# Four-layer transformer kernel: clipping moved from VectorE to GpSimd in a quantised layer, and matrix products of the identity added ahead of the first attention units of the last phase

## The reference

```python
def _act_fake_quant(x, clip_factor):
    scale = jax.nn.sigmoid(clip_factor) * jnp.max(jnp.abs(x)) / QMAX
    return jnp.clip(_ste_round(x / scale), -QMAX - 1.0, QMAX) * scale
...
xq = _act_fake_quant(x, clip_x[0])
gate = jnp.einsum('bsh,ih->bsi', xq, _weight_fake_quant(w_gate))
up = jnp.einsum('bsh,ih->bsi', xq, _weight_fake_quant(w_up))
h = _act_fake_quant(jax.nn.silu(gate) * up, clip_down[0])
return jnp.einsum('bsi,hi->bsh', h, _weight_fake_quant(w_down))
```

## Time and profile before

| what | value |
|---|---|
| runs, median of three | 2119.77 us |
| lowest and highest of them | 2115.42 and 2124.47 us |
| the profiled execution, its own time | 2117.64 us |
| its span, first to last instruction | 2115.9 us |
| PE busy | 1859.6 us, 88% of the span |
| DVE busy | 1486.2 us, 70% |
| ACT busy | 1302.6 us, 62% |
| POOL busy | 616.5 us, 29% |
| mean granted TensorE clock | 0.957 |

### The profile page before, as it was taken

The page is one execution under the profiler, slowest core; times in us unless marked ns, Lnnn a source line. Parts: engine busy times, 40 slices in busy tenths (PEclk is TensorE's granted clock), DMA queues, the critical chain, the costliest instruction groups (busy, mean ns, idle before and its releaser), DMA issues.

```text
span 2115.9 us, 49981 instructions
## 1 busy us (share of the span) xinstructions
PE 1859.6 (88%) x17665; PEld 1511.9 (71%) x17669; DVE 1486.2 (70%) x3873; ACT 1302.6 (62%) x4466; POOL 616.5 (29%) x610
## 2 busy tenths in 40 slices
PE   3998999989999897577898889999999998898879
PEld 2777888878888775455666677787777777677665
DVE  5898887878888785757666675767757565654556
ACT  1987766656667786456577766667666654544432
POOL 0003031322322220034333343254452523233321
PEclk9999999999999999868699999999999999999999
DMA  8013455444644001300000011222222223232351
GB/s 245 17 31 105 126 163 156 134 136 140 181 133 127 26 26 50 110 20 20 30 7 15 7 46 50 83 75 89 79 74 69 76 87 91 71 103 70 110 155 43
DMA packets 128789, 178.44 MB, mean 84 GB/s; under 512 B 10144, under 2 KB 89824, under 8 KB 128288
## 3 DMA queue, kind: packets, MB, share of 16 engines
q1 hardware_dynamic: 120864, 159.51, 25.0%
q0 software_dynamic: 7680, 15.74, 2.4%
HBM read 141.26 MB, written 33.95 MB: 83 GB/s over the span
## 4 chain that ended last, share of the span: by engine, by line
PE 38%; DVE 9%; ACT 6%; issue 4%; POOL 1%; DMA 0%; DVEq 0%; ACTq 0%; SPq 0%
PE ps L1674 5%; PE ps L1959 5%; PE ps L1907 3%; PE ps L1712 3%; PE ps L1900 3%; ACT pb L2108 3%; PE ps L1696 3%; PE ps L1881 2%; PE ps L1703 2%; PE ps L1685 2%; PE ps L1722 1%; DVE nm L2487 1%; PE ps L1730 1%; PE ps L1929 1%; PE ps L1873 1%
## 5 line engine op out<-in xcount | busy, mean ns | idle before, releaser
L2108 ACT ACTIVATE pb<-ps,nm 128x128 f32<-128x128 f32 x1024 | 363.1, 377 | 192.6 <-DVE nm L2487 192.5
L2156 POOL TENSOR_TENSOR pb<-pb,rcs 128x512 f32<-128x512 f32 x256 | 268.3, 1049 | 667.1 <-DVE rcs L2495 666.2
L986 ACT ACTIVATE pb<-pb,nm 128x128 f32<-128x128 f32 x1024 | 312.9, 393 | 30.9 <-DVE nm L1221 29.1
L2512 DVE COPY pt<-ps 128x512 f32<-128x512 f32 x128 | 88.3, 690 | 203.6 <-PE ps L1959 203.4
L2108 ACT ACTIVATION_READ_ACCUMULATOR pb<-ps,nm 128x1 f32 x1024 | 221.3, 216 | 0.0
L2487 DVE TENSOR_REDUCE nm<-ps 128x8 f32<-128x1024 f32 x128 | 155.9, 1218 | 62.2 <-PE ps L1907 39.0
L1959 PE MATMUL ps<-w,pb 128*128 128x128 f32 x1024 | 168.7, 290 | 21.9 <-ACT pt L2116 10.8
L1221 DVE TENSOR_REDUCE nm<-pb 128x8 f32<-128x1024 f32 x128 | 156.2, 1220 | 4.4
L1959 PEld LDWEIGHTS ps<-w,pb 128*128 128x128 f32 x1024 | 122.4, 148 | 46.3 <-ACT pt L2116 20.3
L870 PE MATMUL ps<-w,pb 128*128 128x128 f32 x1024 | 141.8, 280 | 8.2 <-ACT pb L986 7.9
L2116 ACT ACTIVATE pt<-ps 128x512 f32<-128x512 f32 x128 | 76.9, 601 | 94.9 <-PE ps L1959 94.6
(11 more groups left out here) (379 smaller groups left out, 4405.0 us busy)
## 6 DMA issues: line engine op xcount, KB each, us to landing
big<-in_we SPq DMA_DIRECT2D x92, 514.0 KB
big<-in_we SPq DMA_DIRECT2D x109, 384.0 KB
sorted_out<-big SPq DMA_DIRECT2D x27, 256.0 KB
big<-sorted_in SPq DMA_DIRECT2D x7, 960.0 KB, 5.7
sorted_in<-big SPq DMA_DIRECT2D x4, 1472.0 KB, 12.1
big<-sorted_in SPq DMA_DIRECT2D x20, 256.0 KB, 3.8
hidden<-h_all SPq DMA_DIRECT2D x7, 512.0 KB, 3.0
h_all<-hidden SPq DMA_DIRECT2D x7, 512.0 KB, 3.7
```

Source lines behind the costliest of these rows:

```text
L986: m = a.activation(pb[:, n % 2, k * S:(k + 1) * S], pb[:, n % 2, k * S:(k + 1) * S], ACT.Exp, bias=nm[:, n % 2, k:k + 1])
L2108: m = a.activation(pb[:, n % 2, e * S:(e + 1) * S], ps[:, score_bank(n) + half, k * S:(k + 1) * S], ACT.Exp, bias=nm[:, n % 2, e:e + 1], a ...
L2156: g_.tensor_tensor(p4, p4, r4.unsqueeze(2).to_broadcast([P, 4, S]), ALU.mult).then_inc(n2["p_normed"], 1)
L2512: v.tensor_copy(pt[:, p % 2, 4 * S:8 * S], ps[:, BANK_T, :]).then_inc(n2["p_lo"], 1)
```

## The change

The eight clips of the quantised layer leave DVE and become instructions of GpSimd, with the same bounds, the same wait for `x_copied` and the same signal; DVE's wait for `scales` ahead of the first clip goes too. In the third phase a second helper `idle_work` stands in PE's `work`, which issues products of the identity with itself into `BANK_PV` at four places of the first group: ten at `hs` -4, place 0, ahead of the down projection; fourteen at `hs` -3, place 2, ahead of the transposes of y; two at `hs` -2, place 0, ahead of the query projection; and five at `hs` -1, place 1, ahead of the scores of unit 0. They wait for nothing and signal nothing.

```diff
+            @block.gpsimd
+            def _(g_):
+                for j in range(NG):
+                    source = h_all[:, FF_ORDER[j] * NC1, :]
+                    g_.wait_ge(x_copied, j + 1)
+                    g_.tensor_scalar(source, source, MAGIC + QMAX, MAGIC - QMAX - 1.0, ALU.min, ALU.max).then_inc(quantised, 1)
...
-                def clipped(j):
-                    source = h_all[:, FF_ORDER[j] * NC1, :]
-                    v.wait_ge(x_copied, j + 1)
-                    v.tensor_scalar(source, source, MAGIC + QMAX, MAGIC - QMAX - 1.0, ALU.min, ALU.max).then_inc(quantised, 1)
...
-                v.wait_ge(scales, 2)
-                clipped(0)
                 for j, g in enumerate(FF_ORDER):
-                    if j + 1 < NG:
-                        clipped(j + 1)
                     for c, (at, m) in enumerate(CH1):
...
+                def idle_work(count):
+                    for k in range(count):
+                        pe.matmul(ps[:, BANK_PV, k % 4 * P:(k % 4 + 1) * P], ident, ident, start=True, stop=True)
+
                 def work(place, hs):
+                    if hs == L2_AT[0][0] - 4 and place == 0:
+                        idle_work(10)
+                    if hs == L2_AT[0][0] - 3 and place == 2:
+                        idle_work(14)
+                    if hs == L2_AT[0][0] - 2 and place == 0:
+                        idle_work(2)
+                    if hs == L2_AT[0][0] - 1 and place == 1:
+                        idle_work(5)
                     chunk = QK_AT.get(hs)
```

## The result

The changed kernel takes 2098.39 us, the median of 8 runs from 2092.44 to 2100.51. The kernel before, run beside it, takes 2115.57 us, the median of 8 runs from 2106.40 to 2124.47. The ratio is 0.993, with a 95% interval from 0.9913 to 0.9947.

The account below looks back on a forecast made before the run. Bounds: a DVE-ACT ring in the quantised layer's passes, and PE's waits and low clock at the third phase's start. 2117.64 - 9.2 (clips) - 1.1 (identity products) = 2107.3 us, taken as 2108; range 2102 to 2115.

Parts of the forecast that it names:

- The clips: Quantised layer: clips moved to POOL bring passes to 4.38 us, worth -9.2 us, between -8.4 and -9.2.
- the ring: Quantised layer: each pass loops through DVE and ACT (maxima, clip, `rounded`, silu, product, maxima), 5.91 us on average.
- PE's ring: Quantised layer: PE's three chunks, `turn`, ACT's `turned`, PE again; bounds a pass at 4.38 us after the change.
- The price of POOL's clip: Quantised layer: a clip on POOL taken as 0.8 us, covered in later passes; 0.89 us free at the first.
- The rival of a late first clip: Quantised layer: only POOL's first clip is late; 2108 us, or some 2113 with a 6 us first call; chance 0.05.
- a clip longer than a pass: Quantised layer: POOL's clip sets the pass, nothing won from 5.85 us a clip; 2129 us at 7.5; chance 0.03.
- POOL against DVE: Quantised layer: whether working POOL slows DVE's products or maxima; no loss taken, 3.1 us if held; rival's chance 0.08.
- The rival of passes of 4.82 us: Quantised layer: DVE and POOL hold each other, so passes cost 4.82 us; 2110.4 us; chance 0.08.
- The identity products: Start of third phase: raise PE's clock; +0.3 down projection, -0.5 transposes, -0.5 query projection, -0.4 scores: -1.1 us.
- bring nothing: Start of third phase: clock stays low or falls before the transposes; 0 to +2.5 us, 2109.4 us; chance 0.15.
- the clock stays up: Third phase: high clock lasts past the scores, some 6 us beyond the forecast, 2101 us; chance 0.09.
- How the numbers follow: Closing step giving chances and range; low-clock pieces between 934 and 1072 move, allowed 3 us either side.

Follow-up runs that it names:

- e5: Kernel before with the clip kept on DVE but issued a pass earlier, no identity products added: 2101.66 us, ratio 0.9932.
- e7: Changed kernel with two instead of three identity products behind each chunk of the quantised layer: 2102.54 us, ratio 0.9943.
- e2: Kernel before plus only the third-phase identity products, clips staying on DVE: 2121.16 us, ratio 1.0022.
- e8: Changed kernel with fourteen more identity products at `hs` 0 and five at `hs` 1, behind the first scores: 2096.59 us, ratio 0.9919.
- e1: Changed kernel without the third-phase identity products, so only the clips on POOL: 2100.29 us, ratio 0.9944.
- e12: Kernel before, unaltered, profiled a third time: 2114.21 us.
- e9: e1 plus five unread copies on DVE (about 0.9 us) ahead of the third phase: 2112.58 us, ratio 0.9999.
- e10: e1 plus twenty-two small unread copies on DVE (about 2.1 us) ahead of the third phase: 2111.80 us, ratio 0.9995.
- e3: Changed kernel again, unaltered: 2098.79 us, ratio 0.992.
- e6: Changed kernel with four unread copies on DVE (about 1.1 us) ahead of the third phase's first instruction: 2104.07 us, ratio 0.9945.
- e11: e7 and e8 together, on the changed kernel: 2093.23 us, ratio 0.9909.
- e4: Kernel before again, unaltered, a single execution: 2119.62 us.

## Why the prediction was wrong

**The clips: right, one figure by luck.** A pass of 4.38 us was forecast and 4.38 came; seven gave 9.16 us, forecast 9.2. The reason held in both halves: e5 shows that the place in order opened the ring, e7 that PE's ring is what remained. But the 4.38 us were read off the first step, and that step is ACT's. The timeline of ACT after the change has a load of 1.28 us there and `turned` right behind the silu, with no wait for PE; the last row is `turned` of a later pass, which waits for PE:

```profile
840.89 1.28 ACT L1328 ACT_TABLE_LOAD   x1
842.19 1.26 ACT L1328 ACTIVATE hT<-ps,gsc 128x512 f32<-128x512 f32 x2
843.35 0.60 ACT L1309 ACTIVATE pt<-ps 128x512 bf16<-128x512 bf16 x1
...
860.89 0.60 ACT L1309 ACTIVATE pt<-ps 128x512 bf16<-128x512 bf16 x1 [0.76 <-PE ps L1268]
```

In e7, with PE's ring shortened, the first step still takes 4.37 us and the others 3.75 to 3.85. That the first step and PE's ring are equally long is a coincidence.

**The price of POOL's clip: right in effect.** It was taken as 0.8 us and is 0.61. The first clip cost nothing visible. The timeline of POOL after the change shows the first two together:

```profile
837.11 1.31 POOL L1337 TENSOR_SCALAR h_all<-h_all 128x512 f32<-128x512 f32 x2 [7.64 <-ACT h_all L1296]
```

Two in 1.31 us, with no delay inside. The rival of a late first clip is out, and so is that of a clip longer than a pass. The 6 us that the Trainium skill's page "GPSIMD Engine Reference", section "Instruction dispatch", gives for the first call of freshly loaded code did not appear; whether this code had been loaded before, no run here tells.

**POOL against DVE: right for the maxima, untested for the products.** The last five clips all lie beneath DVE's maxima, which take 1.86 us there as before. The Trainium skill's page "SBUF — State Buffer", section "Who interferes with whom", says that a reduction never takes part in the contention, and the trace agrees. Line 1359 takes 1.39 us for two, as before 1.41, but no clip of this trace falls on it, so its case stays open. The rival of passes of 4.82 us is out by the passes themselves.

**The identity products: the sum right, its terms not.** Forecast -1.1 us, measured -0.98. The ten products let the down projection begin 0.50 us later, and DVE's line behind it (2335, before 2325) 0.35 later, forecast +0.3. The transposes gained 0.46, as forecast. But the query projection stayed at the low clock (2.05 us, forecast a gain of 0.5), behind a pause of PE of 2.11 us ahead of the transposes, and the stretch from the scores to the maxima gained 0.9 instead of 0.4: two errors that cancel. The runs alone (e2) could not have told this from the rival "bring nothing". That the clock would fall after the scores was right, though the gap of 3.32 us is not "longer than any gap that the products now fill" (6.35 and 5.27); what counts is what they leave open. e8 shows the gap to be the reason: with it filled, the rival "the clock stays up" holds for unit 0 to 4, with 3.7 us.

**The step that failed** stands under "How the numbers follow": the clock's low pieces behind unit 4 "will fall in other places once all begins 10 us earlier", and "I give that 3 us to either side". The mechanism was named, its size was not worked out. It is 8.7 us in the profiled pair, 5.5 of it from unit 4 to 24, and so the prediction's own last sign, "if the stretch up to 1072 gives back or adds more than 3 us", came true. From the earlier trace rows a bound could have been had: a mean clock of 0.79 over 138 us is 138 x 0.21 x 2 = 58 us at 1.2 GHz, and if PE set the pace in all of them, 29 us would be at stake. How much of that is on the path they don't say. A smaller part of the miss is the starting value. 2108 us with a gain of 10.3 means 2118.3 for the kernel before; the median of its eight runs is 2115.57, and in the later sets of 23, 31 and 23 runs it is 2112.85, 2115.77 and 2111.69. Of the 9.6 us between 2108 and 2098.39, 2.7 are this, and 6.9 a gain of 17.2 instead of 10.3.

What the experiments show of the cause: where the clock is low behind unit 4 makes the 8.7 us (0.79 against 0.84 from unit 4 to 24, with 113.81 and 106.70 busy us of PE for the same work). The identity products aren't needed for it (e1 has the short pattern without them, e2 the long one with them: 136.85 + 166.26), nor are the short passes as such (e12 has long ones and the short pattern). The moment at which the work comes to the third phase is the best candidate. For it speaks that the timed runs of e9 and e10 show nothing of what the passes gain. e9's ratio of 0.9999 and e1's of 0.9944 are 0.0055 or 11.6 us apart, where the copies account for 0.9; the intervals (from 0.9967, to 0.9968) just touch, and the two ran on different chips. In the profiles, too, stretches with the same start have the same length, whatever the kernel. Counted from unit 4, the next stretch at the low clock begins 7.5 us behind it in the profile of before and 7.6 in e9 (unit 4 to 24: 138.29 and 138.38); 8.4 in e1 and 8.5 in e5 (132.10 and 132.13); 9.0 to 9.3 after and in e3, e6, e7, e8 and e11 (132.79 to 132.98). The windows views of before, e9 and e1, in which unit 4 begins at 933.55, 924.52 and 921.13:

```profile
941.00:947.80 6.80, 6.05 (x33) 5.62 (x34) 4.56 (x12) 3.63 (x18) 1.61 (x3) 0.50 0.00 0
```

```profile
932.10:938.90 6.80, 6.12 (x33) 5.62 (x34) 4.50 (x12) 3.62 (x17) 1.61 (x3) 0.50 0.01 2
```

```profile
929.60:936.40 6.80, 6.61 (x34) 5.85 (x35) 4.01 (x11) 3.63 (x16) 1.84 (x2) 0.50 0.01 2
```

Against it as the whole cause speak e2, e4 and e12, where that stretch begins 9.4 us behind unit 4 and which then take 136.85, 140.16 and 132.85 us. There something smaller decides, perhaps a race like the one shown under e12.

What stays open: what the moment of entry is late or early against, so that it could be forecast, and how much of the 9.4 us between e9 and e1 comes from the copies, since two profiles of one kernel, e4 and e12, lie 10.5 us apart there without an edit. A profile shows one execution, but the mean granted clock of each timed run is on record and goes with its time: of e1's twelve, seven took 2093.17 to 2100.46 us at 0.966 to 0.970 and five 2104.37 to 2114.80 at 0.956 to 0.963, while six of e9's ten took 2110.85 to 2122.60 at 0.953 to 0.960. So both kernels seem to have both patterns, in different shares. The short one appeared in all profiles with short passes and no copies ahead of the phase (after, e1, e3, e5, e7, e8, e11) and in e6, the long one in e9, e10 and three of the four with long passes. Whether e6 is slower than the changed kernel is open; its profile is that of the fastest of its twelve runs. The passes of e2 took 41.63 us in its profile, 1.8 more than before, because its first step takes 6.32 us: the granted clock was 0.50 from 839 to 843, in the first pass.

## What to carry to other kernels

When two engines wait for each other once in each pass, look first for an instruction whose input was ready a pass earlier and move it forward in its own engine's order; another engine for it may not be needed. Then ask what ring is left, since products that only keep the clock up can be part of it. Where PE's clock is low in part of the time, a few microseconds ahead, and now and then no change at all, can shift what follows by as much as the change is worth: compare by stages, take several profiles of the kernel before, and widen the range by what the low pieces could cost.

## What was not expected of the hardware

- The same program took 132.85 us from unit 4 to 24 in one execution and 140.16 in another (e12, e4), though both agreed within 0.1 us until 67 us behind unit 0. The first difference is which of DVE and POOL held up the other: DVE's four products took 1.70 us beneath POOL's instruction in e12 and 0.84 in e4, where POOL's took 1.58 instead of 1.06.
- Less than a microsecond of copies went with 9.4 us more further on (e9 against e1, unit 4 to 48), in code that is the same in both; the timed runs point the same way.
- PE can be busy without a pause in the records and the clock still be at 1.2 GHz: in e4 from 1034 to 1038 it was busy for 4.00 of 4.00 us at a granted clock of 0.50.
- The time of one kernel varies with its mean granted clock: beside e1 to e4 the kernel before ran in 2107.87 us at 0.965 and in 2126.06 at 0.957.
- Nineteen products of the identity that compute nothing used shortened unit 0 to 4 by 3.7 us (e8).
